# A transformer layer on 8 cores: weight scans moved among the attention exponentials, per-tile output stores, a looser evacuation wait

## The chip, the cores and the metric

The kernel runs on the 8 cores of one Trainium2 chip, each with the same program on its own rows; the cores don't talk to each other. The time is the device time of the slowest core, in microseconds (us), lower is better.

## The reference, cut to what matters

One layer with two residual steps, each followed by a layer norm over the last axis: grouped-query causal attention (16 query heads, 4 key/value heads, head width 128, 2048 tokens, 4 batches), then a gated feed-forward step whose three weight matrices are made ternary. The scale `s` of each matrix is the mean of the absolute values of the whole matrix, so every weight has to be read once before the first can be quantized.

```python
def ternary_quant(w):
    s = jnp.mean(jnp.abs(w))
    q = jnp.clip(jnp.round(w / s), -1.0, 1.0) * s
    return w + jax.lax.stop_gradient(q - w)
...
x = _layernorm(x + _L0_attn_ref(x, Wq, bq, Wk, bk, Wv, bv), axis=-1)
# ffn: w1q, w3q, w2q = ternary_quant(w1), ternary_quant(w3), ternary_quant(w2)
#      out = (silu(x @ w1q.T) * (x @ w3q.T)) @ w2q.T
x = _layernorm(x + _L0_ffn_ref(x, w1, w3, w2), axis=-1)
```

## The kernel before, in words

Each core takes one batch and half of its rows (1024 rows, in 8 tiles of 128, picked so that causal work is even). Every engine has its own instruction list, written out by hand: a piece of program is handed over with `on("engine", fn)` and stands on its engine behind all pieces handed over earlier, in a block of its own. Engines meet through counting semaphores (`INC` raises one, `W` waits for a count). The stages in the order of time are:

1. **Projections** (L198 to L333). K and V from 2048 rows, then Q head by head from 1024 rows: 40 units. `proj_unit` (L180) lets TensorE fill one of four PSUM tensors (psA, psB, psR, psO in turn) and VectorE evacuate it. Unit u on TensorE waits until `pe`, the count of evacuated units, is u - 1 (L185). The weights of Q come one head at a time by GpSimd's DMA queue (L259).
2. **The scan of w2** (L349): ScalarE takes the absolute value of 16 slabs of 128x5504 with a running sum (`accum_out`), beside stage 1. Each of the 16 is a block of its own.
3. **The scan of w1 and w3** (L359 to L376, "ab2" in the names): 86 slabs of 128x2048 (1024 KB each), loaded through GpSimd's queue (L366) into two buffers in turn, semaphores `la` and `lb`; slab j is loaded once the activation of slab j - 2 is done (`fS`). The loads stand in GpSimd's queue behind all loads of Q's weights. ScalarE's part, `p_ab2_scalar`, is one block with all 86 activations (L374) and stands ahead of the first exponential of attention.
4. **Attention** (L423 to L526): 256 steps, 16 heads (h) by 16 chunks of 128 keys (kc). For each step TensorE makes scores into psA or psB in turn (L436), ScalarE takes the exponential into `ab` (L489), VectorE multiplies one 128x128 corner by the mask (L509), and TensorE adds the row sums into psR (L457) and the output into psO (L464). On TensorE the order is scores of step idx, then sums and output of step idx - 1. Chunks get narrower along a head: 1024 columns at kc 0 and 1, 128 at kc 14 and 15. After kc 15 ScalarE copies psO out (L493) and VectorE copies psR (L514), TensorE transposes it, VectorE takes reciprocals (L519). After every fourth mask (kc 2, 6, 10, 14) VectorE also quantizes a quarter slab of w2 (L416 and L419, `emit_w2p_quarter`). The four quarters of a slab are loaded together by SyncE (L398, 688 KB each), once the slab before is done and its result is being written back (L389, 1376 KB).
5. **Scales, residual, norm** (L530 to L697): `p_fin_vector` (L530) waits for all scans and sums their partials (L532 to L534), which gives the thresholds; then SyncE loads the rows of x (L575), TensorE and VectorE add the attention output, and `emit_ln` (L632) norms 8 tiles one after another, between VectorE and ScalarE. Its first ScalarE piece (L637) is a squaring of 128x2048 with a running sum, in a block of its own.
6. **Feed-forward** (L705 to L941): w1 and w3 are loaded again (L738), quantized on VectorE (L757, L760) and multiplied (L797); w2 comes back quantized (L856) for the second product (L911).
7. **Final norm and store** (L948 to L950): `emit_ln` again, then `emit_store_out` (L618): SyncE waits for the last tile's norm and issues 8 stores of 1024 KB (L622).

The two places in the scan and the store that matter read so:

```python
def p_ab2_scalar(scalar):
    for j in range(NAB2):                      # 86
        W(scalar, "la" if j % 2 == 0 else "lb", 16 * (j // 2 + 1))
        buf = aff(F_AB2 + (j % 2) * 2048, 2048)
        INC(scalar.activation(buf, buf, AF.Abs,
                              accum_out=aff(F_PAR + NEC + j, 1)), "fS", 1)
on("scalar", p_ab2_scalar)
```

Of the kernel before, what the change touches and what calls it, by code (L numbers as in the profile page):

```python
# [80 lines left out]
def _build_nc(debug_stage=None):  # L81
# [18 lines left out]
    cnt = {}  # L100

    with contextlib.ExitStack() as ctx:
# [11 lines left out]
        def INC(instr, name, k=1):  # L114
            instr.then_inc(sems[name], k)
            cnt[name] += k
            return cnt[name]

        def W(eng, name, val):
            if val > 0:  # L120
                eng.wait_ge(sems[name], val)
# [3 lines left out]
        def on(engname, fn):  # L125
            getattr(blk, engname)(fn)

        def abf(c0, n):
            return ab[:, c0:c0 + n]

        def aff(c0, n):
            return af[:, c0:c0 + n]
# [47 lines left out]
        def proj_unit(mm_fn, ev_fn):  # L180
            u = unit[0]
            unit[0] += 1

            def tfun(tensor, u=u, mm_fn=mm_fn):
                W(tensor, "pe", max(0, u - 1))  # L185
                last = mm_fn(tensor)
                INC(last, "pm", 1)
            on("tensor", tfun)

            def vfun(vector, u=u, ev_fn=ev_fn):  # L190
                if u == 0:
                    W(vector, "lc", LC_CONSTS)
                W(vector, "pm", u + 1)
                last = ev_fn(vector)
                INC(last, "pe", 1)
            on("vector", vfun)
# [141 lines left out]
        NAB2 = len(ab2_pieces)  # L338
# [10 lines left out]
        for i in range(NEC):  # L349
            def sfun(scalar, i=i):  # L350
                W(scalar, "ld", LD_CONSTS + 16 * min(i + 2, NEC))
                buf = aff(F_ABS + (i % 2) * 6144, HIDP)
                INC(scalar.activation(buf, buf, AF.Abs,  # L353
                                      accum_out=aff(F_PAR + i, 1)), "fS", 1)
# [12 lines left out]
                                     in_=dsrc[hc]), "la" if j % 2 == 0 else "lb", 16)  # L367
        on("gpsimd", p_ab2_gp)

        def p_ab2_scalar(scalar):  # L370
            for j in range(NAB2):
                W(scalar, "la" if j % 2 == 0 else "lb", 16 * (j // 2 + 1))
                buf = aff(F_AB2 + (j % 2) * 2048, 2048)
                INC(scalar.activation(buf, buf, AF.Abs,  # L374
                                      accum_out=aff(F_PAR + NEC + j, 1)), "fS", 1)
        on("scalar", p_ab2_scalar)  # L376

# [101 lines left out]
        def p_att_scalar_idx(idx):  # L481
            def sfun(scalar, idx=idx):
                h, kc = divmod(idx, 16)
                N = NV[kc] * 128
                ps = psA if kc % 2 == 0 else psB
                W(scalar, "sc", idx + 1)
                if idx >= 16:
                    W(scalar, "av", idx - 15)
                INC(scalar.activation(abf(A_PT + OFF[kc], N), ps[:, 0:N], AF.Exp,  # L489
                                      bias=m16col), "ex", 1)  # L490
                if kc == 15:
                    W(scalar, "av", idx + 1)
                    INC(scalar.activation(abf(A_OFM + h * 1024, 1024), psO[:],  # L493
                                          AF.Copy), "oev", 1)
            on("scalar", sfun)

        for idx in range(256):
            p_att_scalar_idx(idx)
        FS_ABS = FS_PRE + NAB2

        def p_att_vector_idx(idx):
# [28 lines left out]
        def p_fin_vector(vector):  # L530
            W(vector, "fS", FS_ABS)
            vector.reduce_sum(aff(F_P3 + 0, 1), aff(F_PAR + NEC, NHC), AX.X)  # L532
            vector.reduce_sum(aff(F_P3 + 1, 1), aff(F_PAR + NEC + NHC, NHC), AX.X)
            INC(vector.reduce_sum(aff(F_P3 + 2, 1), aff(F_PAR + 0, NEC), AX.X),  # L534
                "fV", 1)
# [79 lines left out]
        on("vector", p_ob_vector)  # L615
        FV_OB = cnt["fV"]

        def emit_store_out(wait_v):  # L618
            def p_st(sync):
                W(sync, "fV", wait_v)  # L620
                for t in range(8):
                    INC(sync.dma_start(out=d_out[t * 128:(t + 1) * 128, :],  # L622
                                       in_=aff(F_X1 + t * 2048, 2048)), "st", 16)
                sync.wait_ge(sems["st"], cnt["st"])
            on("sync", p_st)

        if debug_stage == "x1pre":
            emit_store_out(FV_OB)
            ps_stack2.close()
            return nc  # L630

        def emit_ln(first_wait_v):  # L632
            prev_v = [first_wait_v]
            for t in range(8):
                def sfun(scalar, t=t, pv=prev_v[0]):
                    W(scalar, "fV", pv)
                    INC(scalar.activation(abf(A_SQD, 2048), aff(F_X1 + t * 2048, 2048),  # L637
                                          AF.Square, accum_out=aff(F_LN + 1, 1)),
                        "fS", 1)
                on("scalar", sfun)  # L640

                def vfun(vector, t=t, pv=prev_v[0]):
                    W(vector, "fV", pv)
                    INC(vector.reduce_sum(aff(F_LN + 0, 1), aff(F_X1 + t * 2048, 2048),
                                          AX.X), "fV", 1)
                on("vector", vfun)
                v_sum = cnt["fV"]

                def sfun2(scalar, v_sum=v_sum):
                    W(scalar, "fV", v_sum)  # L650
                    scalar.mul(aff(F_LN + 2, 1), aff(F_LN + 0, 1), INVN)
                    INC(scalar.activation(aff(F_LN + 3, 1), aff(F_LN + 0, 1),
                                          AF.Square, scale=INVN), "fS", 1)
                on("scalar", sfun2)
                s_m = cnt["fS"]

                def vfun2(vector, s_m=s_m):
                    W(vector, "fS", s_m)
                    INC(vector.scalar_tensor_tensor(aff(F_LN + 4, 1), aff(F_LN + 1, 1),
                                                    INVN, aff(F_LN + 3, 1),  # L660
                                                    ALU.mult, ALU.subtract), "fV", 1)
                on("vector", vfun2)
                v_var = cnt["fV"]

                def sfun3(scalar, v_var=v_var):
                    W(scalar, "fV", v_var)
                    INC(scalar.activation(aff(F_LN + 5, 1), aff(F_LN + 4, 1),
                                          AF.Sqrt, bias=epscol), "fS", 1)
                on("scalar", sfun3)
                s_std = cnt["fS"]  # L670

                def vfun3(vector, t=t, s_std=s_std):
                    W(vector, "fS", s_std)
                    rc_done = INC(vector.reciprocal(aff(F_LN + 6, 1),
                                                    aff(F_LN + 5, 1)), "fV", 1)
                    W(vector, "fV", rc_done)
                    INC(vector.tensor_scalar(aff(F_X1 + t * 2048, 2048),
                                             aff(F_X1 + t * 2048, 2048),
                                             aff(F_LN + 2, 1), aff(F_LN + 6, 1),
                                             ALU.subtract, ALU.mult), "fV", 1)  # L680
                on("vector", vfun3)
                prev_v[0] = cnt["fV"]

        emit_ln(FV_OB)
        FV_LN1 = cnt["fV"]

        if debug_stage == "x1":
            emit_store_out(FV_LN1)
            ps_stack2.close()
            return nc  # L690
# [252 lines left out]
        if debug_stage == "x2pre":  # L943
            emit_store_out(FV_FB)
            ps_stack3.close()
            return nc

        emit_ln(FV_FB)  # L948
        FV_LN2 = cnt["fV"]
        emit_store_out(FV_LN2)  # L950
        ps_stack3.close()

    return nc
# [107 lines left out]
```

## Time and profile before

| what | us |
|---|---|
| median of the 2 runs timed | 3102.44 (3093.49 to 3111.39) |
| the profiled execution, its own time | 3100.93 |
| its span on the slowest core (core 4) | 3099.2 |
| spans of the eight cores | 3062.4 to 3099.2 |
| TensorE matmul busy | 1669.1 (54%) |
| ScalarE (ACT) busy | 1001.1 (32%) |
| VectorE (DVE) busy | 807.8 (26%) |
| DMA share, mean rate | 121 GB/s |

The span runs from the first to the last instruction of one core; the execution's own time has 1.7 us around it. No engine is busy for more than about half of the span, so the shares say little by themselves: the stages follow one another and each has its own limit. PE is TensorE, ACT ScalarE, DVE VectorE, POOL GpSimd, SP SyncE.

### The profile page before, as it was taken

The page shows a single profiled execution, that of the slowest core. Times are in us where ns is not written, and L with a number is a line of the kernel's source. Part 1 is how long each engine was busy: PE and PEld are TensorE (multiplying, and loading weights), DVE is VectorE, ACT ScalarE, POOL GpSimd, SP SyncE. Part 2 cuts the span into 40 slices and gives each one's busy share as a digit, 9 for nine tenths or more (in the row PEclk, how much of TensorE's full clock was granted, in tenths as well). Part 3 has the DMA queues.
Part 4 walks back from the last instruction along what each step waited for, and adds up shares of the span by engine and source line. Part 5 has one row for each costly group of instructions (what it writes and reads, how often), then busy time and mean ns, then how long its engine had stood idle before and what let it go on. Part 6 is the DMA issues. An engine that isn't in the chain of part 4 may idle for free.

```text
span 3099.2 us, 19664 instructions; the slowest of 8 cores (3062.4 to 3099.2 us)
## 1 busy us (share of the span) xinstructions
PE 1669.1 (54%) x6824; PEld 712.6 (23%) x6824; DVE 807.8 (26%) x1243; ACT 1001.1 (32%) x969; POOL 61.9 (2%) x120
## 2 busy tenths in 40 slices
PE   0492565000025555555531587887888766778760
PEld 0240222000012222222210333333333322333320
DVE  0020000000013333333345544444444430000013
ACT  0333102444468777878705100000000000110024
POOL 0000000111100000000000000000000000000000
PEclk9996777555556666666655799999999987888885
DMA  9747324666632222212230533333333332111102
GB/s 224 206 181 190 103 34 129 243 234 232 238 122 96 110 110 110 107 74 93 110 127 0 194 119 112 119 122 121 110 121 110 113 120 98 55 54 38 55 18 108
DMA packets 50741, 376.55 MB, mean 121 GB/s; under 512 B 5590, under 2 KB 5846, under 8 KB 16726
## 3 DMA queue, kind: packets, MB, share of 16 engines
q1 hardware_dynamic: 33558, 259.96, 23.2%
q0 software_dynamic: 17088, 115.35, 12.9%
q8 instruction: 57, 0.93, 0.1%
q14 instruction: 38, 0.31, 0.0%
HBM read 361.13 MB, written 39.32 MB: 129 GB/s over the span
## 4 chain that ended last, share of the span: by engine, by line
DMA 33%; PE 25%; DVE 15%; ACT 14%; issue 7%; another core or an unknown queue 4%; SPq 1%; DVEq 0%; ACTq 0%; POOL 0%; POOLq 0%
DMA af<-w_sb 24%; PE pH L911 11%; DVE ab L760 6%; ACT L489 5%; DMA ab<-wq_sb 4%; DVE ab L757 3%; DMA ab<-w2qs 3%; ACT af L374 3%; ACT ab L489 2%; PE psR L457 1%; DVE ab L416 1%; PE psA L320 1%; PE pH L797 1%; PE psB L320 1%
## 5 line engine op out<-in xcount | busy, mean ns | idle before, releaser
L797 PE MATMUL pH<-ab 128*128 128x512 bf16 x2752 | 641.3, 395 | 148.5 <-DVE ab L769 109.7
L457 PE MATMUL psR<-ab 128*128 128x512 bf16 (+3 forms) x384 | 142.3, 433 | 647.7 <-DVE ab L509 646.6
L797 PEld LDWEIGHTS pH<-ab 128*128 128x128 bf16 x2752 | 273.8, 101 | 515.6 <-issue 227.3
L911 PE MATMUL pH<-ab 128*128 128x512 bf16 x1376 | 326.3, 402 | 109.0 <-DMA ab<-w2qs 109.0
L489 ACT ACT_TABLE_LOAD x256 | 328.4, 1283 | 100.7 <-PE psB L436 91.9
L811 ACT ACTIVATE af<-pH,af 128x1024 f32<-128x1024 f32 x43 | 47.9, 1114 | 706.7 <-DVE ab L769 699.3
L509 DVE TENSOR_TENSOR ab<-ab 128x128 bf16<-128x128 bf16 x256 | 55.6, 222 | 705.4 <-ACT ab L489 705.4
L374 ACT ACTIVATE af<-af 128x2048 f32<-128x2048 f32 x86 | 164.2, 1909 | 205.1 <-DMA af<-w_sb 205.1
L757 DVE TENSOR_SCALAR ab<-af 128x2048 bf16<-128x2048 f32 x86 | 110.6, 1286 | 402.7 <-DMA af<-w_sb 402.7
L457 PEld LDWEIGHTS psR<-ab 128*128 128x128 bf16 x384 | 32.9, 105 | 775.9 <-issue 774.8
L911 PEld LDWEIGHTS pH<-ab 128*128 128x128 bf16 x1376 | 139.9, 102 | 291.6 <-issue 148.4
L760 DVE SCALAR_TENSOR_TENSOR ab<-af,ab 128x2048 bf16<-128x2048 f32 x86 | 202.3, 2352 | 9.0
L464 PE MATMUL psO<-ab 128*128 128x512 bf16 (+3 forms) x384 | 148.4, 448 | 0.0
L872 DVE TENSOR_TENSOR af<-pH,af 128x128 f32<-128x128 f32 x128 | 26.8, 282 | 443.9 <-PE pH L927 443.9
L887 ACT ACTIVATE af<-pH,af 128x512 f32<-128x512 f32 x32 | 22.0, 687 | 353.1 <-PE pH L927 352.9
L419 DVE SCALAR_TENSOR_TENSOR ab<-af,ab 128x1376 bf16<-128x1376 f32 x64 | 105.7, 1652 | 7.1 <-DVE ab L416 0.5
L353 ACT ACT_TABLE_LOAD x16 | 20.5, 1283 | 232.2 <-DMA af<-w_sb 232.2
L489 ACT ACTIVATE ab<-psA,af 128x1024 bf16<-128x1024 f32 (+7 forms) x128 | 94.8, 740 | 1.5
L489 ACT ACTIVATE ab<-psB,af 128x1024 bf16<-128x1024 f32 (+7 forms) x128 | 94.8, 740 | 1.5
L209 PE MATMUL psA<-ab 128*128 128x512 bf16 x64 | 16.9, 431 | 119.5 <-DMA ab<-wv_sb 119.5
L353 ACT ACTIVATE af<-af 128x5504 f32<-128x5504 f32 x16 | 76.6, 4790 | 0.2
L436 PE MATMUL psB<-ab 128*128 128x512 bf16 x192 | 75.0, 454 | 0.0
(101 smaller groups left out, 1253.0 us busy)
## 6 DMA issues: line engine op xcount, KB each, us to landing
af<-w_sb POOLq DMA_DIRECT2D x86, 1024.0 KB, 6.3
af<-w_sb SPq DMA_DIRECT2D x86, 1024.0 KB, 4.9
af<-w_sb SPq DMA_DIRECT2D x16, 2752.0 KB, 10.8
af<-w_sb SPq DMA_DIRECT2D x64, 688.0 KB, 8.7
w2qs<-ab SPq DMA_DIRECT2D x16, 1376.0 KB, 5.7
ab<-w2qs SPq DMA_DIRECT2D x16, 1376.0 KB, 6.5
ab<-xkvT POOLq DMA_DIRECT2D x8, 1024.0 KB, 49.6
ab<-wq_sb POOLq DMA_DIRECT2D x16, 512.0 KB, 5.3
```

The costliest lines, as they stand in the source:

```text
L320: last = tensor.matmul(ps[:, b2 * 512:(b2 + 1) * 512], lhs, abf(A_XKV + ec * 1024 + b2 * 512, 512), start=(ec == 0), stop=(ec == NEC - 1))
L353: INC(scalar.activation(buf, buf, AF.Abs, accum_out=aff(F_PAR + i, 1)), "fS", 1)
L374: INC(scalar.activation(buf, buf, AF.Abs, accum_out=aff(F_PAR + NEC + j, 1)), "fS", 1)
L419: INC(vector.scalar_tensor_tensor(qq, st, aff(F_MF + 2, 1), qq, ALU.is_lt, ALU.subtract), "fq", 1)
L436: last = tensor.matmul(ps[:, b2 * 512:b2 * 512 + n2], abf(A_KFM + g * 2048 + kc * 128, 128), abf(A_QFM + h * 1024 + b2 * 512, n2), start=T ...
L457: tensor.matmul(psR[:, b2 * 512:b2 * 512 + n2], ones128, abf(A_PT + OFF[kc] + b2 * 512, n2), start=(kc == 0), stop=stop)
L464: last = tensor.matmul(psO[:, b2 * 512:b2 * 512 + n2], abf(A_VTM + kc * 512 + g * 128, 128), abf(A_PT + OFF[kc] + b2 * 512, n2), start=(kc ...
L489: INC(scalar.activation(abf(A_PT + OFF[kc], N), ps[:, 0:N], AF.Exp, bias=m16col), "ex", 1)
L757: n1 = INC(vector.tensor_scalar(qq, st, aff(F_UC + uc, 1), None, ALU.is_gt), "bq", 1)
L760: INC(vector.scalar_tensor_tensor(qq, st, aff(F_NUC + uc, 1), qq, ALU.is_lt, ALU.subtract), "bq", 1)
L797: last = tensor.matmul(ps[:, b2 * 512:(b2 + 1) * 512], lhs, abf(A_XKV + ec * 1024 + b2 * 512, 512), start=(ec == 0), stop=(ec == NEC - 1))
L911: last = tensor.matmul(ps[:, b2 * 512:(b2 + 1) * 512], lhs, abf(A_G + hc * 1024 + b2 * 512, 512), start=(hc == 0), stop=(hc == NHC - 1))
```

## The change

It has three parts.

1. `proj_unit`: TensorE waits for the evacuation of unit u - 4 rather than of unit u - 2 (`W(tensor, "pe", max(0, u - 3))`).
2. The scan of w1 and w3 on ScalarE: the one block of 86 activations ahead of attention is split into 86 blocks, and one is put behind every third exponential or so: after step idx as many are handed over as make the count `((idx + 1) * 86) // 256`. GpSimd's loads and all other engines' programs of this part stay as they are.
3. `emit_ln` notes VectorE's count after each tile, and the final store waits before each of its 8 DMAs for that tile alone.

```diff
             def tfun(tensor, u=u, mm_fn=mm_fn):
-                W(tensor, "pe", max(0, u - 1))
+                W(tensor, "pe", max(0, u - 3))
...
-        def p_ab2_scalar(scalar):
-            for j in range(NAB2):
+        def emit_ab2_scalar(j):
+            def sfun(scalar, j=j):
                 W(scalar, "la" if j % 2 == 0 else "lb", 16 * (j // 2 + 1))
                 buf = aff(F_AB2 + (j % 2) * 2048, 2048)
                 INC(scalar.activation(buf, buf, AF.Abs,
                                       accum_out=aff(F_PAR + NEC + j, 1)), "fS", 1)
-        on("scalar", p_ab2_scalar)
+            on("scalar", sfun)
...
+        _nab = [0]
         for idx in range(256):
             p_att_scalar_idx(idx)
+            want = ((idx + 1) * NAB2) // 256
+            while _nab[0] < want:
+                emit_ab2_scalar(_nab[0])
+                _nab[0] += 1
...
-        def emit_store_out(wait_v):
+        def emit_store_out(wait_v, per_tile=None):
             def p_st(sync):
-                W(sync, "fV", wait_v)
                 for t in range(8):
+                    W(sync, "fV", per_tile[t] if per_tile else wait_v)
                     INC(sync.dma_start(out=d_out[t * 128:(t + 1) * 128, :],
                                        in_=aff(F_X1 + t * 2048, 2048)), "st", 16)
...
+        ln_tile_done = []
...
                 prev_v[0] = cnt["fV"]
+                ln_tile_done.append(cnt["fV"])
...
-        emit_store_out(FV_LN2)
+        emit_store_out(FV_LN2, per_tile=list(ln_tile_done))
```

On ScalarE, from the last slab of w2 into the first head, the list of before reads as follows. L353 is the scan of w2, L374 that of w1 and w3, L489 the exponential; each branch row ends a block.

```order
L353 ACTIVATE af<-af 128x5504
L126 UNCONDITIONAL_BRANCH
L374 ACTIVATE af<-af 128x2048 x86
L126 UNCONDITIONAL_BRANCH
L489 ACTIVATE ab<-psA,af 128x1024
L126 UNCONDITIONAL_BRANCH
L489 ACTIVATE ab<-psB,af 128x1024
```

The same place in the changed kernel, on the same engine:

```order
L353 ACTIVATE af<-af 128x5504
L126 UNCONDITIONAL_BRANCH
L489 ACTIVATE ab<-psA,af 128x1024
L126 UNCONDITIONAL_BRANCH
L489 ACTIVATE ab<-psB,af 128x1024
L126 UNCONDITIONAL_BRANCH
L489 ACTIVATE ab<-psA,af 128x896
L126 UNCONDITIONAL_BRANCH
L374 ACTIVATE af<-af 128x2048
L126 UNCONDITIONAL_BRANCH
L489 ACTIVATE ab<-psB,af 128x896
```

The 86 scans have left the place ahead of the first exponential, and the first of them now stands behind the third exponential, as a block of its own.

At the end of attention ScalarE had the last exponential, the copy of psO (L493) and then the first norm (L637):

```order
L489 ACTIVATE ab<-psB,af 128x128
L493 ACTIVATE ab<-psO 128x1024
L126 UNCONDITIONAL_BRANCH
L637 ACTIVATE ab,af<-af 128x2048
L126 UNCONDITIONAL_BRANCH
```

In the changed kernel, where L648 is the norm's line:

```order
L489 ACTIVATE ab<-psB,af 128x128
L493 ACTIVATE ab<-psO 128x1024
L126 UNCONDITIONAL_BRANCH
L374 ACTIVATE af<-af 128x2048
L126 UNCONDITIONAL_BRANCH
L648 ACTIVATE ab,af<-af 128x2048
```

The last of the 86 scans stands behind the last copy of psO, so it is the last thing that `p_fin_vector` waits for.

## Rows read from the trace of the kernel before

**Rows 1.** The page: the span, and the chain that ended last, by line.

```profile
span 3099.2 us, 19664 instructions; the slowest of 8 cores (3062.4 to 3099.2 us)
...
DMA af<-w_sb 24%; PE pH L911 11%; DVE ab L760 6%; ACT L489 5%; DMA ab<-wq_sb 4%; DVE ab L757 3%; DMA ab<-w2qs 3%; ACT af L374 3%; ACT ab L489 2%; PE psR L457 1%; DVE ab L416 1%; PE psA L320 1%; PE pH L797 1%; PE psB L320 1%
```

**Rows 2.** Stretches of core 4: scan of w1/w3, attention, final store.

```profile
core 4: us, PE busy (x) PEld busy (x) DVE busy (x) ACT busy (x) POOL busy (x), PEclk, DMA share, GB/s
...
525.00:889.00 364.00, 0.36 (x2) 0.00 (x0) 0.00 (x0) 164.21 (x165) 42.80 (x81) 0.50 0.64 236
889.00:1567.00 678.00, 365.79 (x1282) 143.15 (x1282) 240.99 (x535) 534.31 (x528) 0.00 (x0) 0.64 0.25 96
...
3075.00:3099.00 24.00, 0.00 (x0) 0.00 (x0) 0.00 (x0) 0.00 (x0) 0.00 (x0) 0.50 0.96 350
```

**Rows 3.** Timeline: start us, length, instruction; first scan loads, first scores, first exponential.

```profile
500.18 1.07 POOL L366 DMA_DIRECT2D af<-w_sb  x2
...
524.34 0.59 PE L436 MATMUL psA<-ab 128*128 128x512 bf16 x2 [1.65 <-DVE ab L329]
...
888.97 1.28 ACT L489 ACT_TABLE_LOAD   x1
```

**Rows 4.** Groups of ScalarE by form: busy us, mean ns | idle before, releaser.

```profile
L489 ACT ACT_TABLE_LOAD x256 | 328.4, 1283 | 100.7 <-PE psB L436 91.9 <-PE psA L436 5.0
L374 ACT ACTIVATE af<-af 128x2048 f32<-128x2048 f32 x86 | 164.2, 1909 | 205.1 <-DMA af<-w_sb 205.1
...
L353 ACT ACT_TABLE_LOAD x16 | 20.5, 1283 | 232.2 <-DMA af<-w_sb 232.2
...
L374 ACT ACT_TABLE_LOAD x1 | 1.3, 1283 | 179.5 <-DMA af<-w_sb 179.5
```

**Rows 5.** Timeline of the last norm's first block on ScalarE, and the next.

```profile
3005.11 1.28 ACT L637 ACT_TABLE_LOAD   x1 [3.35 <-DVE af L939]
...
3008.43 1.28 ACT L651 ACT_TABLE_LOAD   x1
```

**Rows 6.** Waits of ScalarE in attention: us in total, times, longest.

```profile
ACT L489 <- PE psB L436: 91.9, 63, 5.2
ACT ab L493 <- PE psO L464: 32.0, 16, 2.0
ACT L489 <- PE psA L436: 5.0, 11, 0.8
```

**Rows 7.** Waits of VectorE in attention, the one for a DMA.

```profile
DVE ab L416 <- DMA af<-w_sb: 39.7, 15, 4.0
```

**Rows 8.** Timeline in the first head: a quantization ahead of a mask, and after.

```profile
898.35 1.65 DVE L419 SCALAR_TENSOR_TENSOR ab<-af,ab 128x1376 bf16<-128x1376 f32 x1
...
902.65 1.28 ACT L489 ACT_TABLE_LOAD   x1 [1.17 <-PE psB L436]
```

**Rows 9.** Timeline at the end of attention.

```profile
1558.03 1.02 ACT L493 ACTIVATE ab<-psO 128x1024 bf16<-128x1024 f32 x1 [2.00 <-PE psO L464]
...
1562.00 0.18 DVE L532 TENSOR_REDUCE af<-af 128x1 f32<-128x43 f32 x1
```

**Rows 10.** Waits of TensorE in the projections, the longest for Q's weights.

```profile
PE psA L320 <- DMA ab<-wq_sb: 70.1, 4, 52.1
```

**Rows 11.** The final stores in the timeline of SyncE's queue.

```profile
3074.53 8.28 SPq L622 DMA_DIRECT2D out<-af  x8
```

**Rows 12.** DMA issues on the page: engine, count, KB each, median us to landing.

```profile
af<-w_sb POOLq DMA_DIRECT2D x86, 1024.0 KB, 6.3
...
w2qs<-ab SPq DMA_DIRECT2D x16, 1376.0 KB, 5.7
```

**Rows 13.** Core 7: its span, its first scores, its exponentials from first to last.

```profile
core 7: 3070.0 us, clock 0.767
...
524.27 0.59 PE L436 MATMUL psA<-ab 128*128 128x512 bf16 x2 [1.65 <-DVE ab L329]
...
L489 ACT ACT_TABLE_LOAD  x256: 1283/1283/1283, 859.3 to 1526.6; - x128
```

More of the change, by code:

```diff
@@ L495, in p_att_scalar_idx @@
             on("scalar", sfun)
+        _nab = [0]
         for idx in range(256):
             p_att_scalar_idx(idx)
+            want = ((idx + 1) * NAB2) // 256
+            while _nab[0] < want:
+                emit_ab2_scalar(_nab[0])
+                _nab[0] += 1
+        while _nab[0] < NAB2:
+            emit_ab2_scalar(_nab[0])
+            _nab[0] += 1
         FS_ABS = FS_PRE + NAB2
@@ L630, in _build_nc @@
             return nc
+        ln_tile_done = []
         def emit_ln(first_wait_v):
+            del ln_tile_done[:]
             prev_v = [first_wait_v]
```

## The prediction

> **What bounds the kernel now.** No engine is full, so I read by stages. The chain that ended last comes first [rows 1]: its largest part, 24%, is the load of weights into `af` ("DMA af<-w_sb"), which holds the scan of w1 and w3 and the feed-forward's own loads. The stretches of the slowest core then tell the two apart [rows 2]. From 525 to 889 us TensorE is busy for 0.36 us and VectorE not at all; ScalarE works 164.2 of 364.0 us, and the DMA engines move 236 GB/s. This is the scan of w1 and w3 alone. The reader should see two things: TensorE has its first scores at 524.34, and the first exponential's block begins only at 888.97 [rows 3], because 86 scans stand ahead of it in ScalarE's list; and the scan itself waits for loads, 205.1 us in all [rows 4]. The scan's first loads leave at 500.18, behind those of Q's weights, so it can't move earlier by itself.
>
> Attention follows, 889 to 1562. ScalarE is busy for 534.3 of the 670.1 us from 888.97 to the end of its last copy (1558.03 + 1.02) [rows 2, 3, 9], TensorE for 366. ScalarE is what limits it: 328.4 us of its time are the 256 table loads of 1.28 us, one ahead of each exponential [rows 4], and it waits 91.9 + 32.0 + 5.0 = 128.9 us for TensorE [rows 6]. The 6.9 us left are gaps of some 0.02 us between instructions. Part of the waiting is VectorE's: a quantization of a quarter slab (1.65 us in its second half) delays the next mask, TensorE's sums behind it and the scores two steps on, and ScalarE waits 1.17 us [rows 8]. In 15 places VectorE also waits for the quarters' loads, 39.7 us in total [rows 7].
>
> At the end, the last norm is done and SyncE issues the stores from 3074.53 on [rows 11], and they take until 3099.2, at 350 GB/s [rows 1, 2]: 24.7 us with nothing beside them.
>
> **Part 1, the looser evacuation wait: 0 us.** TensorE in the projections waits for the DMA of Q's weights, 70.1 us for psA alone with up to 52.1 at once [rows 10]; none of its waits in the view is for VectorE's evacuation of the unit two back, which takes one instruction beside a whole unit of matmuls. Bounds: 0 to 1 us gained. I take 0.
>
> **Part 2, the scan moved into attention.** What is removed: ScalarE no longer has the scan ahead of the first exponential. The loads of slabs 0 and 1 left at 500.18 and TensorE's scores are there at 524.34 + 0.59, so the first block starts at about 525.0 and not at 888.97: 364.0 us taken away.
>
> What is added: 86 blocks in attention. A scan in a block of its own pays a table load. The scan of w2 shows that: 16 blocks, 16 loads [rows 4], while the one block of 86 scans has just one [rows 4]. The same shape with the same running sum in its own block stands in the norm: from 3005.11 to the next block at 3008.43, 3.32 us [rows 5]. So 86 x 3.32 = 285.5 us of ScalarE, of which 85 x 1.28 = 109 are new work, and the rest is the 164 us of before. All of it stands on the engine that limits attention.
>
> What it hides: while ScalarE scans for 3.32 us, TensorE and VectorE go on. A scan stands behind every third exponential and a quantization behind every fourth mask, so between a quantization and the exponential three steps on there is nearly always a scan. It covers the wait of 1.17 us and its like. What it doesn't cover: the copy of psO, which waits for the sums of the same step (2.0 us each time [rows 6]); only where a scan stands behind kc 14 does VectorE get its quantization done early, one head in three, which makes 32 into about 27. The wait at kc 1 stays in two heads of three. Of the 97 us for psB and psA I leave 12 us for those.
>
> What it collides with: the 86 loads of 1 MB now fall into attention, one per 10 us, where the DMA engines are a quarter busy [rows 2]. A load lands in 6.3 us [rows 12] and has nearly two intervals, 20 us, so ScalarE shouldn't wait for it. But at the start of each slab of w2, 2.82 MB of quarters and 1.41 MB of result move together while VectorE will soon want them; it waits 39.7 us / 15 = 2.6 us there now [rows 7]. One or two scan loads fall into that stretch and take 1.05 MB / 350 GB/s = 3.0 us each at the rate of the stores [rows 2]; one or two scans also push VectorE's need back by 3.3 us each. About even, so the 2.6 us stay and a scan nearby hides most; I leave 8 us over 16 heads. The sum of waits left: 27 + 12 + 8 = 47. Bounds: none left, 0; all left, 128.9. At the rows' end for the loads, see the second rival.
>
> Attention of ScalarE: 534.3 + 6.9 + 285.5 + 47 = 873.7 us. It ends at 525.0 + 873.7 = 1398.7 with the last scan, and `p_fin_vector` starts there. Before it started at 1562.0 [rows 9]: 163.3 us earlier. That the last scan stands last costs about 1 us of it, since VectorE's reciprocals end 3 us after the copy of psO anyway, and it is in the sum.
>
> After that nothing is changed up to the store; the stages behind are shifted as a whole.
>
> **Part 3, per-tile stores.** Seven stores leave while later tiles are normed. The last leaves at the same point and has the DMA engines to itself. A 1376 KB write lands in 5.7 us [rows 12]; 8.4 MB at 350 GB/s gives 3.0 us for one of 1 MB. Bounds 3.0 and 5.7 us, I take 5.5, since a landing has a fixed part. 24.7 - 5.5 = 19.2 us gained. The seven others are hidden by the norm, which takes 8.7 us per tile (3074.53 less 3005.11, by 8) [rows 5, 11]; nothing waits behind them on SyncE.
>
> **Sum.** 3099.2 - 163.3 - 19.2 = 2916.7 us on core 4. Core 7 is shorter, 3070.0, but its scan was shorter too: 859.3 - 524.9 = 334.4 us taken away against 364.0 [rows 13], which gives 3070.0 - (182.5 - 29.6) = 2917.1. So the cores meet, and it doesn't matter which is last. With 1.7 us around the span, 2918.6, and 1 for the spread of eight: 2919 us. The profiled execution had 3100.9, and the median is 3102.4, so no shift is made for that. 2% of it is 62 us, about what a measurement of this kernel can tell from no change.
>
> **A rule against it.** Blocks of Abs and of Exp alternate now: 172 changes from one function to the other. The rows show a table load of 1.28 us per block and the next block 0.02 us after the last, at the norm too [rows 5]; at 888.97 an exponential follows a scan with one load [rows 3]. The Trainium skill, "ScalarE: Activation LUTs", section "What ACT_TABLE_LOAD costs", says that every switch to a different set costs the load of 1283 ns plus a drain of about 1380 ns. By that rule, if the two functions load different sets, an estimate of 172 x 1.38 = 237 us would come on top, and the sum would be 3156. The trace agrees with the load and shows no drain so far.
>
> **Rivals.**
> 1. *The switch has a price (slower).* Place: ScalarE in attention, at each change between scan and exponential. Priced as a second load at each, 172 x 1.28 = 220 us, it gives 2919 + 220 = 3139 us, slower than before. It decides from 183 / 172 = 1.06 us per change on. For it: nowhere in the trace do the two alternate. Against it: the one change at 888.97 shows nothing [rows 3]. 4%.
> 2. *The loads collide.* If the quarters and two scan loads move at only the 236 GB/s of the scan's stretch [rows 2], 6.3 MB take 26.8 us against the some 15 us that VectorE gives them; less the 3.3 that a scan hides, 8 us per head, 128 in all: 3047 us. For it: two queues feed the same 16 engines. Against it: 350 GB/s at the end. 7%.
> 3. *No wait is hidden.* The chain of mask, sums and scores stays as late relative to ScalarE: 82 us more, 3001 us. Against it: TensorE is at 54% in attention and ScalarE the longer. 7%.
> 4. *No table load per scan.* The compiler keeps one table for both: 109 us less, 2810 us. Against it: 256 loads for one and the same function [rows 4]. 2%.
>
> **How the numbers follow.** My forecast has 80%, with 2888 to 2968 as its range: below, most waits gone (47 less is 2872) is less likely than above, where the loads collide in part. This range leaves 20% to the rivals, and it is the range I give. Faster by over 2% (below 3040): the forecast, rivals 3 and 4 and some of rival 2, 91%. Within 2%: the rest of rival 2 and most of rival 1, 7%. Slower: 2%.
>
> **What would show it.** The first exponential's table load at about 525; 86 table loads on the scan's line; attention's ScalarE busy near 820 us of 874; its waits for psB and psA down from 97 to some 20, those for psO at 27; VectorE's wait for the quarters near 40; no wait of ScalarE for the scan's loads; the last store about 5.5 us from the end. It is wrong if ScalarE's gaps between blocks grow beyond 0.02 us (rival 1), if VectorE's wait for `w_sb` passes 100 us (rival 2), or if the feed-forward stages, which I take as unchanged, last otherwise.

## The result, and the profile after

The changed kernel takes 2939.2 us (median), 3111.4 for the kernel before beside it; the ratio is 0.944 with a 95% interval of 0.942 to 0.947. The forecast was 2919, range 2888 to 2968. The profiled execution took 2941.4, on core 4 again as the slowest, with the cores between 2911.1 and 2939.6. An 8-core program is now and then some per cent slower, whatever the kernel; the medians hold such runs, the ratios don't.

Attention of core 4 in the changed kernel, as a stretch; the columns are those of [rows 2]:

```profile
529.80:1420.50 890.70, 398.60 (x1278) 148.27 (x1276) 243.24 (x528) 817.02 (x786) 45.10 (x84) 0.58 0.49 172
```

The stretch from 525 to 889 of [rows 2], with TensorE and VectorE idle, has no counterpart any more. Attention starts at 529.8 and is longer, and ScalarE fills 92% of it. The 86 scans and their table loads, from the groups by form (as [rows 4]):

```profile
L489 ACT ACT_TABLE_LOAD x256 | 328.4, 1283 | 233.7 <-PE psA L436 201.7 <-PE psB L436 28.1
L374 ACT ACTIVATE af<-af 128x2048 f32<-128x2048 f32 x86 | 164.2, 1910 | 1.0
L374 ACT ACT_TABLE_LOAD x86 | 110.3, 1283 | 1.5
```

The single table load of the scan has become 86, of which 85 are new: 109 us. And the scan's 205.1 us of waits for its loads are gone: 1.0 us is left. The waits of ScalarE in attention, which answer to [rows 6] (us in total, times, longest):

```profile
ACT L489 <- PE psA L436: 201.7, 18, 191.3
ACT L489 <- PE psB L436: 28.1, 28, 3.5
ACT ab L493 <- PE psO L464: 25.7, 16, 2.0
```

And the one of VectorE for a DMA, as [rows 7]:

```profile
DVE ab L416 <- DMA af<-w_sb: 48.1, 15, 5.6
```

The 191.3 in the first row is the wait ahead of the very first exponential, which is before attention, so psA stands at 10.4. With the 28.1 and the 25.7, in all 64.2 us are left of 128.9. The timeline shows how a scan stands between two exponentials, with gaps of 0.02 us:

```profile
536.42 1.01 ACT L489 ACTIVATE ab<-psA,af 128x896 bf16<-128x896 f32 x1
537.45 1.28 ACT L374 ACT_TABLE_LOAD   x1
538.74 1.91 ACT L374 ACTIVATE af<-af 128x2048 f32<-128x2048 f32 x1
540.56 0.19 ACT L374 ACTIVATION_READ_ACCUMULATOR af<-af 128x1 f32 x1
540.76 1.28 ACT L489 ACT_TABLE_LOAD   x1
```

One block is 3.31 us, from 537.45 to 540.76. The end of attention (as [rows 9]) and the last store (as [rows 11]) in the timeline:

```profile
1418.51 1.91 ACT L374 ACTIVATE af<-af 128x2048 f32<-128x2048 f32 x1
...
1420.62 0.20 DVE L540 TENSOR_REDUCE af<-af 128x1 f32<-128x43 f32 x1 [0.39 <-ACT af L374]
...
2935.41 0.33 SPq L630 DMA_DIRECT2D out<-af  x1
```

`p_fin_vector` starts 141.4 us earlier than before (1562.0 less 1420.6), and 4.2 us pass from the last store's issue to the end of the span, 24.7 before.

### The profile page after: what moved, and what is told of

It is laid out like the page before. It is cut to its first block, busy times and chain, and to the rows that moved or that the text cites. A ratio compares the mean times of both kernels' runs of the same rounds, so it can differ in the third digit from the quotient of the medians.

```text
span 2939.6 us, 19754 instructions; the slowest of 8 cores (2911.1 to 2939.6 us)
## 1 busy us (share of the span) xinstructions
PE 1720.4 (59%) x6824; PEld 722.5 (25%) x6824; DVE 811.0 (28%) x1243; ACT 1110.5 (38%) x1054; POOL 62.6 (2%) x120
## 3 DMA queue, kind: packets, MB, share of 16 engines
q0 software_dynamic: 17088, 115.35, 13.9%
## 4 chain that ended last, share of the span: by engine, by line
DMA 27%; PE 26%; ACT 17%; DVE 14%; issue 10%; another core or an unknown queue 4%; SPq 1%; DVEq 0%; ACTq 0%; POOL 0%; POOLq 0%
DMA af<-w_sb 18%; PE pH L923 12%; DVE ab L772 7%; ACT L489 6%; DMA ab<-wq_sb 5%; DVE ab L769 4%; ACT ab L489 3%; DMA ab<-w2qs 3%; ACT L374 2%; ACT af L374 2%; PE psB L320 1%; PE psA L320 1%; PE psR L320 1%; PE psO L320 1%
## 5 line engine op out<-in xcount | busy, mean ns | idle before, releaser
L809 PE MATMUL pH<-ab 128*128 128x512 bf16 x2752 | 643.5, 396 | 145.3 <-DVE ab L781 109.1
L457 PE MATMUL psR<-ab 128*128 128x512 bf16 (+3 forms) x384 | 153.3, 464 | 467.5 <-DVE ab L517 466.5
L489 ACT ACT_TABLE_LOAD x256 | 328.4, 1283 | 233.7 <-PE psA L436 201.7
L923 PE MATMUL pH<-ab 128*128 128x512 bf16 x1376 | 339.3, 414 | 100.0 <-DMA ab<-w2qs 100.0
L374 ACT ACTIVATE af<-af 128x2048 f32<-128x2048 f32 x86 | 164.2, 1910 | 1.0
L464 PE MATMUL psO<-ab 128*128 128x512 bf16 (+3 forms) x384 | 161.5, 485 | 0.0
L353 ACT ACT_TABLE_LOAD x16 | 20.5, 1283 | 239.7 <-DMA af<-w_sb 239.7
L374 ACT ACT_TABLE_LOAD x86 | 110.3, 1283 | 1.5
L489 ACT ACTIVATE ab<-psA,af 128x1024 bf16<-128x1024 f32 (+7 forms) x128 | 94.8, 741 | 1.5
L489 ACT ACTIVATE ab<-psB,af 128x1024 bf16<-128x1024 f32 (+7 forms) x128 | 94.8, 741 | 1.5
L209 PE MATMUL psA<-ab 128*128 128x512 bf16 x64 | 17.0, 432 | 121.3 <-DMA ab<-wv_sb 121.3
L436 PE MATMUL psA<-ab 128*128 128x512 bf16 x192 | 80.8, 485 | 1.7 <-DVE ab L329 1.7
## 6 DMA issues: line engine op xcount, KB each, us to landing
af<-w_sb SPq DMA_DIRECT2D x16, 2752.0 KB, 12.2
```

The costliest lines, as they stand in the source:

```text
L374: INC(scalar.activation(buf, buf, AF.Abs, accum_out=aff(F_PAR + NEC + j, 1)), "fS", 1)
L436: last = tensor.matmul(ps[:, b2 * 512:b2 * 512 + n2], abf(A_KFM + g * 2048 + kc * 128, 128), abf(A_QFM + h * 1024 + b2 * 512, n2), start=T ...
L457: tensor.matmul(psR[:, b2 * 512:b2 * 512 + n2], ones128, abf(A_PT + OFF[kc] + b2 * 512, n2), start=(kc == 0), stop=stop)
L464: last = tensor.matmul(psO[:, b2 * 512:b2 * 512 + n2], abf(A_VTM + kc * 512 + g * 128, 128), abf(A_PT + OFF[kc] + b2 * 512, n2), start=(kc ...
L809: last = tensor.matmul(ps[:, b2 * 512:(b2 + 1) * 512], lhs, abf(A_XKV + ec * 1024 + b2 * 512, 512), start=(ec == 0), stop=(ec == NEC - 1))
L923: last = tensor.matmul(ps[:, b2 * 512:(b2 + 1) * 512], lhs, abf(A_G + hc * 1024 + b2 * 512, 512), start=(hc == 0), stop=(hc == NHC - 1))
```

## The experiments

All are run on 8 cores and compared with the kernel before on the same chip.

**The parts one by one.** First part 2 alone: the changed kernel with `max(0, u - 1)` and `emit_store_out(FV_LN2)` put back.

> The change with part 2 alone (86 scan blocks among the exponentials); the evacuation wait and the single store wait stand as before. Theory (364 us of ScalarE's list taken from ahead of attention, 86 blocks of 3.32 us put in, of which the waits hide some 70 us): nearly all of the gain is here, the time is the changed kernel's plus the 20 us of the stores, so about 0.951 of before, with 86 table loads on the scan's line. Rival (the parts help one another, or the looser wait carries some of it): a ratio at least 0.01 away from that, above 0.96.

Measured: ratio 0.956, interval 0.950 to 0.963. That is halfway between the theory's 0.951 and the rival's 0.96, and the interval holds both, so the times don't decide. The trace does. The 86 table loads are there, and attention lasts 872 to 882 us on the eight cores, 867 to 881 in the changed kernel (here and below from the first to the last exponential of psA, the last but one of all). Cores 6 and 7, the longest, had their first scores only at 550.0 and 543.2 us, the six others at 517.6 to 527.5; those two make the execution long. On cores 0 to 3 the spans are 2937.4 to 2947.5 us, on average 21 us more than the changed kernel's 2911.1 to 2931.7, about what the stores give (20 us, below). So this part carries the gain, and nothing is seen of the parts helping one another.

Part 3 alone:

```diff
-        emit_store_out(FV_LN2)
+        emit_store_out(FV_LN2, per_tile=list(ln_tile_done))
```

> Part 3 alone: the final store waits per tile; the scan stands ahead of attention in one block. Theory: the last store lands 3 to 5.5 us after its issue in place of 24.7, so 19 to 22 us less than before, ratio 0.993. Rival (the stores of earlier tiles slow the norm on VectorE and ScalarE, which read and write the same memory): the norm's period of 8.63 us per tile grows by up to 1 us, and the gain falls below 12 us, ratio 0.996 or more.

Measured: ratio 0.985, interval 0.978 to 0.992. That would be 25 us or more, above the theory's 19 to 22 and not to be put down to the stores. Part of it is chance in what is compared: in many executions one pair of cores lags (more on this in the last section), and where none does, this kernel takes 3052.7 and 3055.3 us and the kernel before 3076.5, 21 to 24 us apart. The trace is sharper. On its slowest core, with a span of 3091.2, the norm's blocks follow one another as before, and the last store ends 4.1 us after its issue:

```profile
3017.66 1.28 ACT L640 ACT_TABLE_LOAD   x1 [3.35 <-DVE af L943]
...
3026.30 1.28 ACT L640 ACT_TABLE_LOAD   x1 [1.80 <-DVE af L680]
...
3034.94 1.28 ACT L640 ACT_TABLE_LOAD   x1 [1.80 <-DVE af L680]
...
3087.09 0.33 SPq L622 DMA_DIRECT2D out<-af  x1
```

From the first of these blocks to the last store's issue it is 69.4 us for 8 tiles with stores running beside them, as without (3074.53 less 3005.11, [rows 5, 11]). The rival is out: the stores cost the norm nothing, and by the trace they give 20 us.

Part 1 alone:

```diff
-                W(tensor, "pe", max(0, u - 1))
+                W(tensor, "pe", max(0, u - 3))
```

> Part 1 alone: TensorE waits for the evacuation four units back in place of two. Theory: no wait of TensorE in the projections was for an evacuation, so 0 to 1 us, ratio 1.000. Rival (units in a row now overlap an evacuation that held them): the stretch from the first K matmul to the first scores gets shorter by 5 us or more, ratio 0.998 or less.

Measured: ratio 1.003, interval 0.999 to 1.007. From the first K matmul to the first scores it takes 398.5 us on core 2 (119.0 to 517.5), 398.0 before (119.3 to 517.3). On cores 0 to 5 the difference to before lies between -6.0 and +5.7 us. Cores 6 and 7 take 440.1 and 435.9 us, before 396.2 and 403.7, at a granted clock of 0.67 and 0.68 from 300 to 520 us where the others have 0.77 to 0.80. So there is no gain, as the waits of TensorE had it.

**Does a switch of function have a price, and what makes a table load?** One run puts each scan into the block of the exponential ahead of it (`ab2_body` has the wait and the activation of one scan):

```diff
+            for j in range((idx * NAB2) // 256, ((idx + 1) * NAB2) // 256):
+                ab2_body(scalar, j)
...
-            want = ((idx + 1) * NAB2) // 256
-            while _nab[0] < want:
-                emit_ab2_scalar(_nab[0])
-                _nab[0] += 1
```

> The changed kernel, but each scan stands in the block of the exponential ahead of it, not in one of its own (256 blocks on ScalarE in attention in place of 342). Theory (a table load is put in once per block, since exponential and absolute value share a table): the 86 loads on the scan's line vanish, 110 us of ScalarE; the shorter scans hide some 15 us less, so some 95 us less than the changed kernel, ratio to before about 0.914. Rival (the two functions need different tables, and each change costs a load wherever it stands): as many table loads as in the changed kernel, ratio 0.944.

Measured: ratio 0.939, interval 0.934 to 0.943. Half of the theory holds: the 86 table loads are gone and no other came, so exponential and absolute value share a table and a load is put in once per block. But only 17 us (by the ratios) to 24 us (by the medians) came of 110. The waits of its slowest core in attention say where the rest went, ScalarE's first:

```profile
ACT L484 <- PE psA L432: 196.3, 13, 188.2
ACT L484 <- PE psB L432: 127.2, 27, 11.5
```

and VectorE's for a DMA:

```profile
DVE ab L412 <- DMA af<-w_sb: 132.0, 15, 12.3
```

VectorE waits 132 us for the quarters of w2 (48 in the changed kernel), 8.8 at each of 15 slabs, and ScalarE takes nearly all of it over through mask, sums and scores (psB 127 for 28). The median landing of a quarter's load went from 11.3 to 14.0 us on that core (6). On cores 0 and 1 VectorE waited only 80 and 82 us, and their attention took 806 and 809 us against 845 to 857 on the others. This looks like the collision of the second rival, covered in the changed kernel by the length of its scan blocks; runs below test it.

The other run leaves the blocks and puts Silu in place of Abs, since by the run above Abs and Exp share a table:

```diff
-                INC(scalar.activation(buf, buf, AF.Abs,
+                INC(scalar.activation(buf, buf, AF.Silu,
```

> The changed kernel with the scan's function Silu in place of Abs, everything else alike, so the scales of w1 and w3 are not those of the reference. [...] Theory (a load costs 1.28 us whatever the set, as the rows show between blocks): the time is that of the changed kernel, 2930 to 2940 us, with gaps of 0.02 us between blocks. [...]

Measured: 2946.6 us (2936.8 to 2956.3), ratio 0.953, interval 0.939 to 0.966. The timeline of its slowest core, where each of these loads stands at a change of function:

```profile
701.29 1.28 ACT L374 ACT_TABLE_LOAD   x1
702.59 1.91 ACT L374 ACTIVATE af<-af 128x2048 f32<-128x2048 f32 x1
704.40 0.19 ACT L374 ACTIVATION_READ_ACCUMULATOR af<-af 128x1 f32 x1
704.61 1.28 ACT L489 ACT_TABLE_LOAD   x1
705.90 1.01 ACT L489 ACTIVATE ab<-psB,af 128x896 bf16<-128x896 f32 x1
```

The load is 1.28 us and the gaps 0.02 us, the same as with Abs, and attention takes 867 to 881 us, as in the changed kernel. The two executions timed are 7 us above the expected 2930 to 2940 on average; 237 us more, as in the prediction's rule, is out. That Silu and Exp lie in different tables isn't shown by any run; that neither alternation costs more than its load is.

**How large is the collision in the changed kernel?** Only two of the 86 scan loads are issued:

```diff
-            for j in range(NAB2):
+            for j in range(2):
...
-                W(scalar, "la" if j % 2 == 0 else "lb", 16 * (j // 2 + 1))
+                W(scalar, "la" if j % 2 == 0 else "lb", 16)
```

> The changed kernel with only the first two of the 86 scan loads issued; all 86 scans run on what lies in their two buffers, so the scales of w1 and w3 are not those of the reference. Theory (in the changed kernel the collision of loads is small): VectorE's wait for the quarters falls from 48 to under 15 us on the slowest core, because a scan or two more give the loads more time, ScalarE's waits for psA, psB and psO from 64 to some 50, and the time by 5 to 15 us, ratio to before 0.940. Rival (the scan loads cost attention more than the waits show): 40 us or more gained, ratio 0.932 or less.

Measured: ratio 0.948, interval 0.939 to 0.957, 2927.8 us. On its slowest core VectorE's wait is down to a fifth:

```profile
DVE ab L416 <- DMA af<-w_sb: 9.6, 9, 2.1
```

ScalarE waits 10.0 us for psA (203.0 less the first 193.0), 15.3 for psB and 25.7 for psO: 51 us. On core 4, the slowest of the changed kernel, it is 51 us too, for 64 there. The rival, 40 us or more, is out. The gain of 5 to 15 us doesn't show in the ratio, which is no lower than the 0.944, only in the waits: the scan's loads cost about 13 us.

Then the order of SyncE's queue was changed, so that each quarter is loaded as soon as its own buffer is free, with the write-back behind:

```diff
             for ec in range(NEC):
-                if ec >= 1:
-                    W(sync, "fq", FQ_MF + 2 * (4 * ec))
-                    w2p_ld[("out", ec - 1)] = INC(
-                        sync.dma_start(out=d_w2q[ec - 1], in_=abf(A_W2QS, HIDP)),
-                        "ld", 16)
                 for quar in range(4):
...
+                if ec >= 1:
+                    W(sync, "fq", FQ_MF + 2 * (4 * ec))
+                    w2p_ld[("out", ec - 1)] = INC(
+                        sync.dma_start(out=d_w2q[ec - 1], in_=abf(A_W2QS, HIDP)),
+                        "ld", 16)
...
-                W(vector, "ld", w2p_ld[("in", 4 * (q // 4) + 3)])
+                W(vector, "ld", w2p_ld[("out", ec - 1)] if ec >= 1
+                  else w2p_ld[("in", 3)])
```

In the changed kernel, with scans in blocks of their own:

> The changed kernel with SyncE's order of the w2 quarters changed (each quarter loaded a slab ahead, the write-back behind the loads), scans in blocks of their own. Theory (in the changed kernel the collision with the quarters is small and costs the slower pairs of cores 5 to 15 us): VectorE's wait for w_sb goes to near 0, ScalarE's for psB from 28 to 15, attention from first to last exponential 868 us on all cores in place of 866 to 881, time 5 to 12 us below the changed kernel in the same call. Rival (the quarters' loads cost nothing here, since scans cover their wait): no difference, within 2 us.

Beside it the changed kernel once more:

> The changed kernel itself once more, to stand beside the two others on the same chip. Both theories: ratio 0.944 as before, within its interval, some 2930 to 2940 us.

Measured: 0.946 (0.941 to 0.952) against 0.947 (0.940 to 0.955), 2934.1 and 2936.3 us. By time that is no difference, and the 5 to 12 us of the theory are too few for these times to show or to rule out. In the traces VectorE no longer waits for these loads, and attention takes 867 to 871 us on all cores, 873 to 881 in the repeat. So the theory holds for the waits. Its slowest core's waits of ScalarE are the floor without collision:

```profile
ACT L490 <- PE psA L437: 206.2, 22, 194.0
ACT ab L494 <- PE psO L465: 23.7, 15, 2.0
ACT L490 <- PE psB L437: 16.3, 25, 0.9
```

12.2, 16.3 and (with the one that lies past the window) 25.7: 54 us.

The same edit in the run with the scan in the exponential's block, where the collision was large:

> The run before (scan in the exponential's block) with SyncE's order changed: each quarter of w2 is loaded once its own buffer is free, one slab ahead, and the write-back of the slab comes behind these loads, not ahead of them. So 0.7 MB + 1.4 MB move between two slabs in place of 4.2 MB. Theory (there VectorE waited 80 to 132 us for the quarters, since the shorter scans gave the loads less time, and ScalarE took over nearly all of it): VectorE's wait for w_sb falls below 40 us, ScalarE's for psB from 127 to some 25, and the time to 2930 - 95 = 2835 us, ratio 0.914. Rival (the stretch is bound by the rate of all transfers, 156 MB in 850 us and more on pairs of cores that share a memory): the wait moves to the scan's loads or stays, and the ratio stays at 0.935 or above.

Measured: ratio 0.905, interval 0.899 to 0.911, 2799.6 us; better than expected. On its slowest core VectorE has no wait for a DMA in attention, and ScalarE's waits are

```profile
ACT L485 <- PE psA L433: 199.8, 14, 191.8
ACT ab L489 <- PE psO L461: 25.7, 16, 2.0
ACT L485 <- PE psB L433: 11.5, 18, 0.9
```

8.0 + 25.7 + 11.5 = 45 us. Attention takes 738 to 742 us, on average 128 less than in the changed kernel with the same edit: all 110 us of the table loads, 9 of waits (54 less 45), and the rest from scans and exponentials that now overlap by their last 0.1 us. So the gain that was missing with the scan in the exponential's block had gone to VectorE's waits for the quarters, not to the blocks. How much of these waits comes from the scan's loads running beside the quarters, and how much from the shorter time alone, stays open: no run took the scan's loads out of that kernel.

**What the table loads cost in all.** The whole of ScalarE's attention as one block (the edit is shown against the run with the scan in the exponential's block):

```diff
-        for idx in range(256):
-            def sfun(scalar, idx=idx):
-                att_scalar_body(scalar, idx)
-            on("scalar", sfun)
+        def p_att_scalar(scalar):
+            for idx in range(256):
+                att_scalar_body(scalar, idx)
+        on("scalar", p_att_scalar)
```

> All of ScalarE's attention, 256 exponentials, 16 copies and 86 scans, in one block; the order of the instructions is that of the changed kernel. Theory (table loads are put in per block): one table load in place of 342, ScalarE's busy time in attention falls from 817 to some 380 us, and attention is bound by the chain from TensorE through VectorE and by the quarters' loads: 600 to 680 us in place of 885, the time 2650 to 2730 us, ratio 0.855 to 0.88. VectorE's wait for the quarters grows beyond 132 us. Rival (the loads of 156 MB bound attention): no less than 156 MB / 236 GB/s = 660 us, or the table loads stay.

Measured: 2800.9 us, ratio 0.903, interval 0.893 to 0.914: less than expected. One table load is left of 342, but attention takes 714 to 753 us, since VectorE waits 198 to 239 us for the quarters. Two rows of the timeline of its slowest core, on VectorE and on ScalarE:

```profile
726.41 0.94 DVE L412 TENSOR_SCALAR ab<-af 128x1376 bf16<-128x1376 f32 x1 [17.96 <-DMA af<-w_sb]
...
731.83 0.90 ACT L484 ACTIVATE ab<-psB,af 128x768 bf16<-128x768 f32 x1 [19.05 <-PE psB L432]
```

A wait of VectorE of 18.0 us comes out as one of ScalarE of 19.1: the faster ScalarE gets, the less time the loads have, and the more of it is waited for. With the quarters a slab ahead:

> All of ScalarE's attention in one block, and the quarters a slab ahead. Theory (in the one-block run ScalarE's 400 us of waits were 200 to 237 us of VectorE's wait for the quarters, passed on; without them the chain of mask, sums and scores bounds attention): VectorE's wait for w_sb under 30 us, attention 540 to 580 us in place of 715 to 753, time 2590 to 2640 us, ratio 0.835 to 0.85. Rival (156 MB at some 236 GB/s bound it): attention no shorter than 660 us, ScalarE waits for the scan's loads, time above 2700 us.

Measured: 2636.2 us (2618.1 to 2674.3), ratio 0.846, interval 0.842 to 0.850. This is the version that beats both. Attention of its slowest core as a stretch, columns as in [rows 2]:

```profile
525.00:1090.00 565.00, 316.96 (x1242) 138.64 (x1241) 229.37 (x506) 346.84 (x429) 48.68 (x82) 0.73 0.78 265
```

and there the waits for a DMA, VectorE's:

```profile
DVE ab L413 <- DMA w2qs<-ab: 52.5, 15, 5.3
```

and ScalarE's:

```profile
ACT af L373 <- DMA af<-w_sb: 11.5, 10, 2.2
```

Attention takes 548 to 588 us. VectorE's wait for `w_sb` is gone (0.3 us at most), but 30 to 69 us have come for the write-back of the slab, which now comes last; the DMA engines are at 78% and 265 GB/s, and ScalarE begins to wait for scan loads. No engine is full. ScalarE waits 206 us for TensorE, which waits 225 us for VectorE's masks, which wait 235 us for exponentials: the chain of a step, as the theory had it. How much of it is the loads' doing no run shows.

## Why the prediction was right, and by how much not

**What was taken away.** 364 us were to go. The first block of attention starts at 529.86 where 525.0 was said. That is 4.9 us off, and not seen to come from the change: the first scores come between 513.0 and 529.2 us on the eight cores, between 516.3 and 524.3 before, and part 1 alone shows no shift on its cores 0 to 5.

**What was added.** Right: 86 blocks, 86 table loads, 3.31 us each for 3.32, ScalarE's busy time 817.0 where 534.3 + 285.5 less gaps had been put. All of it lies on the path.

**What it hides.** Of the waits 47 us were to be left and 64.2 are. This is the term that was mis-sized:

| waits of ScalarE left in attention, us | predicted | changed kernel, core 4 | quarters early |
|---|---|---|---|
| psO | 27 | 25.7 | 25.7 |
| psA and psB, TensorE's own chain | 12 | 38.5 with the next row | 28.5 |
| psB, the quarters' loads | 8 | in the row above | 0 |

The copy of psO came out as said. The step that failed is "I leave 12 us for those", the wait at kc 1 in two heads of three, with nothing at the other chunks. Counted by chunk in the timeline of core 4, kc 1 is left with 5.1 us in 6 of 16 heads, less than was put. But 16.0 us stand where none were left for: 10.0 at kc 2, 7, 8 and 9, where 13.9 had been waited before and were taken as hidden, and 6.0 at kc 3, 4 and 6, where nothing had been waited. And kc 5, where before 58.8 of the 96.9 us lay, has 17.3; with the quarters early it has 4.1, so the loads cost 13 us there where 8 had been put (the table's difference is 10, since the other chunks have 24.4 us in that run and 21.1 in this one).

Why waits come up at new chunks: the prediction took TensorE's instructions to last as before. They didn't. In attention the granted clock is 0.58 of full speed where it was 0.64 [rows 2], nearer to the lower level of 1.2 GHz, and TensorE's busy time is 398.6 us where it was 365.8. The row sums and the output on the page, two rows from before and two from the changed kernel:

```profile
L457 PE MATMUL psR<-ab 128*128 128x512 bf16 (+3 forms) x384 | 142.3, 433 | 647.7 <-DVE ab L509 646.6
L464 PE MATMUL psO<-ab 128*128 128x512 bf16 (+3 forms) x384 | 148.4, 448 | 0.0
...
L457 PE MATMUL psR<-ab 128*128 128x512 bf16 (+3 forms) x384 | 153.3, 464 | 467.5 <-DVE ab L517 466.5
L464 PE MATMUL psO<-ab 128*128 128x512 bf16 (+3 forms) x384 | 161.5, 485 | 0.0
```

The same 384 matmuls take 8% and 9% longer. With the scan in the exponential's block and the quarters early, the granted clock in attention is 0.61, TensorE is busy for 373.3 us, and psA and psB are down to 19.5 us, though ScalarE gives TensorE less time there. That fits the clock as the cause of part of the 16 us; it is argued from these rows, and no run held the clock and changed the rest.

**The stores.** 19.2 us predicted, 24.7 - 4.2 = 20.5 measured; one store with the engines to itself took 4.2 us and not 5.5.

**The cores.** It was said that they would meet, since the cores with the longest scan lose the most. They did so only in part: core 7 ended 29.2 us ahead of core 4 before and 20.2 after, and the spread of the eight went from 36.8 us to 28.5. Of the 20.2 us, 16.2 were there at the first scores (513.0 on core 7, 529.2 on core 4), which both cores had at 524.3 before. So it did matter which core is last. That core 7's sum, 2917.1, was met to 2.3 us (2919.4) is luck: its first scores came 11.3 us earlier than before, and its attention was longer than put.

**Sum.** 4.9 + 17.2 - 1.3 on core 4, and 2.3 more from `p_fin_vector` to the last store (1514.8 for 1512.5): 2916.7 + 23.1 = 2939.8, where the span is 2939.6. The larger misses have one sign and don't cancel, so the forecast's standing within its range isn't luck.

**The rivals.** The price of a switch of function: out, with Abs and with Silu. The loads collide: a small term in the changed kernel, some 13 us where 128 would have been needed. But VectorE's wait for the same loads ruled as soon as the blocks got shorter, which no step had said. No wait hidden: out, 64.7 of 128.9 us are gone. No table load per scan: out, 86 are there.

## What to carry to other kernels

Work that stands alone ahead of a stage is worth moving into it even where the stage's own engine is the full one, as long as what goes away (here 364 us, most of it waiting for loads) is more than what the engine gets (285 us less the waits that it fills). Look at how instructions are grouped into blocks before counting their time: a table load per block was 328.4 + 110.3 us of ScalarE here, more than all exponentials and scans together (189.6 + 164.2). And when an engine is made faster, ask which load had been hidden by its slowness: the fix of the load was worth nothing that the times could show in the changed kernel, and moved the ratio from 0.939 to 0.905 once the table loads of the scans were gone.

## What was not expected of the hardware

- Alternating two functions on ScalarE, 172 times, costs the table load of 1.28 us each time and nothing beside it, with gaps of 0.02 us. The Trainium skill, "ScalarE: Activation LUTs", section "What ACT_TABLE_LOAD costs", gives a drain of about 1380 ns on top for every switch to a different set. No run here shows one, but none is sure to test it either: Abs and Exp were seen to share a table, and whether Silu and Exp do wasn't tested.
- In the scan ahead of attention one pair of cores is slower than the others, and it is another pair in other profiles. From its first to its last activation the scan takes 374 to 376 us on cores 4 and 5 in the kernel before, on cores 0 and 1 in the run of part 1 alone and on cores 2 and 3 in that of part 3 alone, and 346 to 350 us on all others. Why is open. (Cores 6 and 7 of the run of part 1 alone reach attention late too, but for the projections: their scan starts at 544.3 and 537.4 us, that of the others at 503.1 to 511.9, and is as short as theirs.)
- TensorE's granted clock in attention fell from 0.64 to 0.58 when ScalarE's scans spread the same matmuls over more time, and rose to 0.73 in the fastest run, where they lie closer.
